# Two-stage cross-attention: two 512x512 products made from seven block products instead of eight, with mixed context sums on GpSimd and their low parts on VectorE

## What is computed

```
q = x wq^T;  k = c wk^T;  v = c wv^T
x1 = x + alpha * (softmax(q k^T / sqrt(512)) v) wo^T
g = g_w c + g_b;  phi = phi_w c + phi_b;  theta = theta_w x1 + theta_b
W = theta^T phi / 512
y = (W g^T)^T
out = bn_gamma * (w_w y + w_b - bn_mean) / sqrt(bn_var + 1e-5) + bn_beta + x1
```

## Time and profile before

| | |
|---|---|
| median of 3 runs | 388.72 us |
| profiled execution: span from first to last instruction | 386.3 us |
| outside that span, against the median | 2.4 us |
| TensorE busy | 381.0 us |
| VectorE busy | 310.8 us |
| ScalarE busy | 205.4 us |
| GpSimd busy | 3.7 us |

### The profile page before, as it was taken

How to read it: one execution, slowest core, us unless ns; L and a number is a source line. 1 busy time by engine, 2 the same in 40 slices (tenths; PEclk the granted TensorE clock), 3 DMA queues, 4 the chain that set the end, 5 groups by cost and what they waited for, 6 DMA issues and landing times.

```text
span 386.3 us, 5597 instructions
## 1 busy us (share of the span) xinstructions
PE 381.0 (99%) x1776; PEld 318.6 (82%) x1776; DVE 310.8 (80%) x595; ACT 205.4 (53%) x441; POOL 3.7 (1%) x7
## 2 busy tenths in 40 slices
PE   8999999999999999999999999999999999999995
PEld 5888878888888888888888888888888888888885
DVE  4999779987599776996689866996779875996786
ACT  3477568533664267543665257452665346552553
POOL 0001000000000000000000000000000000000000
PEclk9999999999999999999999999999999999999999
DMA  8995842486375646556383556565375564043423
GB/s 242 382 331 188 285 133 54 158 296 225 116 256 145 238 141 211 182 171 217 109 271 112 214 170 198 189 198 188 123 219 181 191 190 136 15 121 144 151 87 110
DMA packets 58059, 70.37 MB, mean 182 GB/s; under 512 B 5056, under 2 KB 47936, under 8 KB 54976
## 3 DMA queue, kind: packets, MB, share of 16 engines
q1 hardware_dynamic: 56144, 67.21, 53.2%
q10 hardware_dynamic: 1904, 3.02, 2.5%
HBM read 51.32 MB, written 18.89 MB: 182 GB/s over the span
## 4 chain that ended last, share of the span: by engine, by line
PE 97%; DMA 1%; DVE 1%; ACT 0%; issue 0%; SPq 0%
PE bank L367 23%; PE bank L368 23%; PE bank L369 23%; PE bank L421 8%; PE bank L440 7%; PE bank L407 5%; PE bank L429 4%; PE bank L462 2%; PE bank L466 1%; DMA xb<-w_k 1%; DVE xb L1143 0%; DVE xb L1138 0%; PE bank L393 0%; ACT theta_hi L621 0%; ACT t_sides L621 0%
## 5 line engine op out<-in xcount | busy, mean ns | idle before, releaser
L367 PE MATMUL bank<-ov_hi,c_sides 128*128 128x512 f32 x128 | 50.0, 391 | 0.0
L368 PE MATMUL bank<-c_sides,qk_hi 128*128 128x512 f32 x128 | 49.9, 390 | 0.0
L369 PE MATMUL bank<-c_sides,qk_lo 128*128 128x512 f32 x128 | 49.9, 390 | 0.0
L368 PE MATMUL bank<-ov_lo,c_sides 128*128 128x512 f32 x128 | 49.9, 390 | 0.0
L367 PE MATMUL bank<-c_sides,qk_hi 128*128 128x512 f32 x128 | 49.8, 389 | 0.0
L369 PE MATMUL bank<-ov_hi,c_sides 128*128 128x512 f32 x128 | 49.8, 389 | 0.0
L621 ACT ACTIVATE t_sides<-bank 128x512 fp32r<-128x512 f32 x32 | 19.0, 594 | 37.2 <-PE bank L369 37.2
L421 PE MATMUL bank<-t_sides,xT_hi 128*128 128x512 f32 x128 | 31.9, 391 | 0.0
L877 DVE TENSOR_TENSOR vo_lo<-bank,vo_hi 128x512 fp32r<-128x512 f32 x32 | 21.8, 685 | 11.8 <-ACT vo_hi L621 10.9
L621 ACT ACTIVATE probs<-bank 128x512 f32<-128x512 f32 x16 | 9.4, 585 | 37.9 <-PE bank L429 37.9
L367 PEld LDWEIGHTS bank<-ov_hi,c_sides 128*128 128x128 f32 x128 | 24.1, 188 | 5.2 <-DVE wg_sides L877 0.4
(11 more groups left out here) (148 smaller groups left out, 820.9 us busy)
## 6 DMA issues: line engine op xcount, KB each, us to landing
cT_raw<-ctx_t SPq DMA_DIRECT2D x8, 1024.0 KB, 4.8
xT_raw<-x_t SPq DMA_DIRECT2D x8, 1024.0 KB, 5.1
c_raw<-ctx_n SPq DMA_DIRECT2D x8, 1024.0 KB, 6.5
xb<-x SPq DMA_DIRECT2D x16, 512.0 KB, 4.2
out<-xb SPq DMA_DIRECT2D x14, 512.0 KB, 2.8
gram_moved<-gram_blocks SPq DMA_DIRECT2D x16, 256.0 KB, 2.3
gram_blocks<-gram_moved SPq DMA_DIRECT2D x64, 64.0 KB, 2.0
moved<-blocks SPq DMA_DIRECT2D x16, 256.0 KB, 2.3
```

Source lines behind the costliest of these rows:

```text
L367: pe.matmul(dst, ahi, bhi, start=(k == 0), stop=False)
L368: pe.matmul(dst, ahi, blo, start=False, stop=False)
L369: mm = pe.matmul(dst, alo, bhi, start=False, stop=(k == k_tiles - 1))
```

## The change

Both products are made with two-by-two blocks of 256 in seven block products, M1 to M7 (the scheme of Strassen in Winograd's form), instead of eight. The two batches of a pair stand side by side as C11, C12 (upper half of the hidden dimension, batches 0 and 1) and C21, C22 (lower half).

- qk and ov are kept as seven blocks: three pure ones and four sums, made at the start by `weight_blocks` on VectorE (seven steps for each weight) and `pure_blocks` and `sum_block` on ScalarE. The low parts of ov's sums are made on GpSimd.
- For each pair GpSimd makes four sums of context blocks, T1 = C12 - C11, N2C = T1 - C22, T3 = C22 - C12, N4C = N2C + C21 (`mixes`), in the memory of c_raw, after the context sums. ScalarE makes their high parts, VectorE their low parts (`mix_part`). Both products use them.
- Each block product is 12 matmuls of 256 columns. M1, M6, M7 and M4 accumulate in one chain bank. ScalarE copies M1 to a seed bank, to which M2 is added (`copy_chain`), and copies M5 to SBUF (`keep_join`). VectorE adds the chain to it twice: `join` writes a PSUM bank, `join_side` the side block in SBUF.
- TensorE waits for all four low parts of t before a pair. delta(0) needs three of the blocks of vo.
- x1 and vo share their memory, theta and pT too.
- load_cT waits for GpSimd's last sum, load_c for the last low part of the sums; load_c stands behind load_xT.
- At the start the high part of w_o moves from VectorE to ScalarE, and GpSimd makes the low parts of phi_w and theta_w.

The diff, cut to its core:

```diff
+FIRST_SUMS = 4
 BLOCKS = P // SQUARE
 SCALE = float(H) ** -0.5
+PRODUCTS = 7
+M1, M2, M3, M4, M5, M6, M7 = range(PRODUCTS)
+A11, A12, S4, A22, S1, N2, S3 = range(PRODUCTS)
+T1, N2C, T3, N4C = range(4)
+MIXED_SIDE = {M4: N4C, M5: T1, M6: N2C, M7: T3}
...
-        x1 = split("x1", [P, 2, KL, H])
+        x1 = vo
+        mix = split("mix", [P, 4, KS, S])
...
-        theta = split("theta", [P, 2, H])
-        qk = split("qk", [P, KH, H])
-        ov = split("ov", [P, KH, H])
+        theta = [t[:].rearrange("p b x n -> p b (x n)") for t in pT]
+        qk = split("qk", [P, PRODUCTS, KH // 2, H // 2])
+        ov = split("ov", [P, PRODUCTS, KH // 2, H // 2])
...
+        mix_raw = c_raw[:].rearrange("p b k (c s) -> p (b k) c s", c=KS)
+        sums_raw = xb[:].rearrange("p b t (c n) -> p (b t) c n", c=2)
+        side_raw = blocks[:, 1].rearrange("p j x a -> p (j x a)").rearrange("p (c n) -> p c n", c=2)
+        vo_side, tT_side = gram_raw[:, 0], probs[:, 1]
...
+        VO_CHAIN, VO_JOIN, VO_SEED = 2, 3, 6
+        TT_CHAIN, TT_JOIN, TT_SEED = 0, 1, 4
...
             load_xT(0)
+            sp.wait_ge(cT_lo, 2)
+            sp.wait_ge(mix_made, 4)
+            load_cT(1)
+            sp.wait_ge(mix_lo, 4)
             load_c(0)
...
                 if prefetch:
-                    if not first:
-                        sp.wait_ge(c_summed, four[8])
-                        load_c(p + 2)
                     sp.wait_ge(cT_lo, two[4])
-                    load_cT(p + 2)
+                    sp.wait_ge(mix_made, four[8])
+                    load_cT(ahead)
...
                     sp.wait_ge(xT_lo, two[4])
-                    load_xT(p + 2)
+                    load_xT(ahead)
+                    sp.wait_ge(mix_lo, four[8])
+                    load_c(ahead)
...
-            def t_tile(m):
-
-                product(bank[TT_BANK[m]][:].rearrange("p (b s) -> p b s", b=2), lambda k: cut(qk, every, k, tile(m)),
-                        lambda k: cut(cT, every, k),
-                        KH).then_inc(tT_done, 1)
+            def context(i, kt):
+
+                if i in MIXED_SIDE:
+                    return cut(mix, every, MIXED_SIDE[i], kt)
+                k, b = {M1: (kt, 0), M2: (2 + kt, 0), M3: (2 + kt, 1)}[i]
+                return cut(cT, every, k, b)
+
+            def half_product(dst, lhsT, rhs, opens):
+
+                for n in range(2):
+                    for kt in range(2):
+                        (ahi, alo), (bhi, blo) = lhsT(n, kt), rhs(n, kt)
+                        at = dst[:, n * S:(n + 1) * S]
+                        pe.matmul(at, ahi, bhi, start=(opens and n == 0 and kt == 0), stop=False, skip_group_check=True)
+                        pe.matmul(at, ahi, blo, start=False, stop=False, skip_group_check=True)
+                        mm = pe.matmul(at, alo, bhi, start=False, stop=(kt == 1), skip_group_check=True)
+                return mm
+
+            def t_product(i, to_bank, opens=False):
+
+                half_product(bank[to_bank], lambda n, kt: cut(qk, every, i, kt, tile(n)),
+                             lambda n, kt: context(i, kt), opens).then_inc(tT_done, 1)
+
+            def v_product(i, to_bank, opens=False):
+
+                half_product(bank[to_bank], lambda n, kt: [t[:, tile(n)] for t in context(i, kt)],
+                             lambda n, kt: cut(ov, every, i, kt), opens).then_inc(vo_done, 1)
...
-            pe.wait_ge(qk_lo, KH)
+            pe.wait_ge(qk_lo, 1)
+            pe.wait_ge(qk_summed, 4)
             pe.wait_ge(cT_lo, 2)
-            both_rows(0)
-            t_tile(0)
-            pe.wait_ge(ov_lo, 2)
-            both_rows(1)
-            pe.wait_ge(ov_lo, KH)
-            t_tile(1)
+            t_product(M1, TT_CHAIN, opens=True)
+            pe.wait_ge(qk_sum_lo, 1)
+            pe.wait_ge(mix_lo, 1)
+            t_product(M5, TT_JOIN, opens=True)
+            pe.wait_ge(tT_copied, 1)
+            pe.wait_ge(qk_sum_lo, 2)
+            pe.wait_ge(mix_lo, 2)
+            t_product(M6, TT_CHAIN)
+            pe.wait_ge(qk_lo, 3)
+            t_product(M2, FIRST_TT_SEED)
+            gram_rows(0, 0, FIRST_GRAM_BANK)
+            pe.wait_ge(tT_joined, 1)
+            pe.wait_ge(qk_sum_lo, 3)
+            pe.wait_ge(mix_lo, 3)
+            t_product(M7, TT_CHAIN)
+            pe.wait_ge(ov_lo, 3)
+            pe.wait_ge(ov_summed, 4)
+            gram_rows(0, 1, FIRST_GRAM_BANK)
+            for i in range(KS):
+                gram_rows(1, i, FIRST_GRAM_BANK)
+            pe.wait_ge(qk_sum_lo, 4)
+            t_product(M3, TT_JOIN)
+            pe.wait_ge(tT_joined, 2)
+            pe.wait_ge(mix_lo, 4)
+            t_product(M4, TT_CHAIN)
+            pe.wait_ge(wg_factor_lo, 2)
             pe.wait_ge(gram_read, 1)
-            t_tile(2)
-            pe.wait_ge(gram_read, 2)
-            t_tile(3)
-            pe.wait_ge(wg_factor_lo, 2)
-            pe.wait_ge(tT_lo, 2)
             combine_w_g()
...
-                pe.wait_ge(tT_lo, four[3])
+                two, four = counts(pe, p, 2, [1, 2, 3, 4]), counts(pe, p, 4, range(-2, 9))
+                pe.wait_ge(tT_lo, four[4])
                 pe.wait_ge(xT_lo, two[2])
-                if not first:
+                if first:
+                    pe.wait_ge(gram_read, 2)
+                else:
                     pe.wait_ge(out_made, four[-2])
-                high_scores(0, range(KH - 1))
-                pe.wait_ge(tT_lo, four[4])
-                high_scores(0, [KH - 1])
...
+                v_product(M1, VO_CHAIN, opens=True)
+                if not first:
                     pe.wait_ge(phi_turned, p + 1)
-                for st in range(KS):
-                    values(0, st)
+                v_product(M5, VO_JOIN, opens=True)
+                pe.wait_ge(vo_copied, two[1])
+                v_product(M6, VO_CHAIN)
+                v_product(M2, VO_SEED)
+                pe.wait_ge(vo_joined, two[1])
+                v_product(M7, VO_CHAIN)
...
+                pe.wait_ge(vo_joined, two[2])
+                v_product(M4, VO_CHAIN)
+                v_product(M3, VO_JOIN)
+                pe.wait_ge(vo_lo, four[3])
...
+                t_product(M1, TT_CHAIN, opens=True)
+                pe.wait_ge(mix_lo, four[5])
+                t_product(M5, TT_JOIN, opens=True)
+                pe.wait_ge(x1_made, four[4])
                 theta_rows(0, [four[1], four[2]])
-                pe.wait_ge(x1_made, four[4])
-                t_tile(1)
+                pe.wait_ge(tT_copied, two[3])
+                pe.wait_ge(mix_lo, four[6])
+                t_product(M6, TT_CHAIN)
+                t_product(M2, TT_SEED)
...
+                pe.wait_ge(tT_joined, two[3])
+                pe.wait_ge(mix_lo, four[7])
+                t_product(M7, TT_CHAIN)
...
+                pe.wait_ge(tT_joined, two[4])
+                pe.wait_ge(mix_lo, four[8])
+                t_product(M4, TT_CHAIN)
+                t_product(M3, TT_JOIN)
...
+            def copy_chain(to_bank, from_bank, done, count, copied):
+                act.wait_ge(done, count)
+                act.activation(bank[to_bank][:], bank[from_bank][:], ACT.Identity).then_inc(copied, 1)
+
+            def keep_join(side, from_bank, done, count, copied):
+                act.wait_ge(done, count)
+                act.activation(side, bank[from_bank][:].rearrange("p (n s) -> p n s", n=2), ACT.Identity).then_inc(copied, 1)
...
             act.wait_ge(ov_done, KH)
-            for m in OV_ORDER:
-                hi(ov[0][:, m, :], bank[KH + m][:], ov_hi, scale=row[:, ROW_ALPHA:ROW_ALPHA + 1])
+            mix_part(T1, 1)
+            mix_part(N2C, 2)
+            act.wait_ge(qk_summed, 4)
+            pure_blocks(ov, KH, ov_done, ov_side, ov_hi, scale=row[:, ROW_ALPHA:ROW_ALPHA + 1])
+            mix_part(T3, 3)
+            mix_part(N4C, 4)
+            copy_chain(FIRST_TT_SEED, TT_CHAIN, tT_done, 1, tT_copied)
+            keep_join(tT_side, TT_JOIN, tT_done, 2, tT_copied)
...
+                copy_chain(VO_SEED, VO_CHAIN, vo_done, seven[1], vo_copied)
                 exp(1)
-                vo_part(0, 0)
+                keep_join(vo_side, VO_JOIN, vo_done, seven[2], vo_copied)
+                if not last:
+                    c_sums(loads[32], batches=[0])
+                vo_part(0, HALF[0], VO_SEED, seven[4])
+                pT_part(0)
+                if not last:
+                    c_sums(loads[32], batches=[1])
+                vo_side_part()
+                if last:
+                    t1_part(0)
+                vo_part(0, HALF[1], VO_CHAIN, seven[6])
                 if first:
                     xT_part(0, loads[32])
-                vo_part(0, 1)
-                if first:
-                    xT_part(1, loads[32])
-                pT_part(0)
+                vo_part(1, HALF[0], VO_JOIN, seven[7])
+                pT_part(1)
...
+            def join(side, join_bank, chain_bank, done, count, kept, copied, joined):
```

(96 more changed lines are left out.)

345 lines of the change are left out of this document (175 added, 170 removed).

## The result

The changed kernel takes 445.12 us (median of 4 runs, 442.37 to 447.7) against 388.55 us before in the same batch: ratio 1.145, 95% interval 1.140 to 1.150. The direction was forecast, the size was not: 428.0 was the point and 442 the upper end of the range. The profiled execution took 442.37 us, the shortest of the four, with a span of 440.6 us, 54.3 us more than the 386.3 us before. The other three have spans of 442.8 to 444.8 us and no trace, so what they have more is not explained here.

A forecast was written before the change was run, and what follows sets the result against it. TensorE, 99% busy, was taken to bound the kernel before, VectorE and its waits after. 388.7 + 17.7 (start) + 4.6 (pair 0) + 15.1 (six steady pairs) + 1.8 (last pair) = 427.9 us; point 428, range 406 to 442.

The forecast's parts named there:

- T1 at 33.3: At the start: GpSimd's first sum follows directly behind its reduction, which ended at 31.7, and is made at 33.3 us.
- rival D: GpSimd's sums hold up VectorE's two-input SBUF steps: 0.8 to 1.6 us in 7 pairs, 2 at the start; 438 us, chance 0.17.
- the walk: Steps followed in written order; in a steady pair 40.7 us of VectorE work plus 6.0 idle give 46.7 us.
- B: Rival: waits shorter than walked, pair 45.0 us, start +11, pair 0 +3, last +1; 408 us, chance 0.18.
- C: Rival: joins hide, TensorE's floor sets the pair, 1.8 us less in 8 pairs, start +11 at most; 385.3 us, chance 0.05.
- TensorE: Both products, 84 matmuls of 256 columns each instead of 48 of 512: 1.8 us less a pair, floor 42.4 us.
- rival E: Matmuls of 256 columns cost more than 0.119 us, for example 0.14: 3.5 us a pair of TensorE; 440 us, chance 0.05.
- VectorE's amount: In a pair: eight more steps of 512 columns at 0.60 us, raising VectorE from 35.84 to 40.7 us.
- GpSimd's sum: A two-input sum of 512 columns on GpSimd: taken as 1.6 us, between 1.0 and 3.2.
- The start: Up to pair 0: GpSimd's sums behind the reduction hold ScalarE and VectorE; pair 0 starts at 59.5 instead of 41.84, +17.7 us.
- VectorE's list alone: At the start, were the GpSimd wait gone, VectorE's steps would still put pair 0 at about 53 us, +11.
- Pair 0: First pair, with t1 rows and sums in its second half: last low part of t at 50.5 against 45.9, +4.6 us.

The follow-up runs named there:

- e4: Kernel before with each tile of the two products cut from 12 matmuls of 512 columns to 21 of 256, part of the contraction left out: 380.57 us, ratio 0.980.
- e7: Kernel before with 21 matmuls of 256 columns a tile (part of the contraction left out) and eight more unused VectorE steps a pair: 396.06 us, ratio 1.018.
- e5: Changed kernel with GpSimd's pair sums cut to 2 columns and ScalarE's side block ahead of the second half of the context sums: 430.85 us, ratio 1.108.
- e2: Changed kernel with GpSimd's four sums of a pair made of 2 columns instead of 512, the rest left out: 436.27 us, ratio 1.119.
- e3: Changed kernel with ScalarE's side block moved ahead of the second half of the context sums, nothing left out: 441.91 us, ratio 1.137.
- e9: Kernel before, full-width matmuls kept, with eight more VectorE steps of 512 columns a pair whose result is unused: 398.66 us, ratio 1.026.
- e1: Changed kernel with GpSimd's reduction over partitions moved behind the sums and ov's low parts at the start, nothing left out: 433.52 us, ratio 1.119.

## Why the prediction was off

The direction was right and the sum was 17.2 us short. Three of its steps failed. The sums at the start were put right behind the reduction ("T1 at 33.3"), and it took 7.18 us more to go back to an ordinary step. GpSimd's hold-up of VectorE stood as rival D and at nothing in the sum; it costs some 4.9 us in the loop and 2.2 in pair 0. And the walk had no term for TensorE's granted clock after a long wait, which costs some 1 us at the end of the start and 1 in pair 0. Rivals B and C are out: a late pair is 47.5 us, not 45.0 or less.

**The pair, in steps.** The experiments take a late pair apart: 44.24 before; 42.68 with the narrow matmuls (e4, −1.56); 44.9 with eight steps on VectorE (e7, +2.2); 45.8 with the rest of the change, but without the hold-up and with the side block first (e5, +0.9); 46.8 with ScalarE's order as written (e2, +1.0); 47.5 with GpSimd's full sums (+0.7). The +0.9 of e5 over e7 is what is left over: the joins' waits, ScalarE's copies and the rest of the order have no experiment of their own. The steps depend on the order in which they are taken: e3 shows the side block's order worth 0.2 with the hold-up there, e5 shows it worth 1.0 without.

**TensorE** was put at −1.8 us a pair (the prediction's own 10.90 and 10.03 give 1.74); it is −1.56 where TensorE sets the time. The 0.119 us for a matmul of 256 columns held (in the steady pair after they start at 226.63, 226.75 and 226.87), so rival E is out. That the saving would be lost once VectorE is full was right, and e7 and e9 measure it: 0.8 left.

**VectorE's amount** was put at 40.7 us; the window shows 41.70. Two steps stretched from 0.69 to 1.46 and 1.49 are 1.6 us of record; e2, where they are not stretched, has 40.30 in the pair from 211.51. The step that writes PSUM, for which there had been no row, starts at 252.52 and the next at 253.12: 0.60, as taken.

**The walk through the pair** gave 6.0 us of idle time. The trace has, in the pair from 215.7, 1.92 at the scores (1.4 was walked), 0.17 for phi (1.0), 0.54 for the exponentials (0.65), 0.78 and 1.03 for the two half blocks (0.85 and 1.1), 0.32 for the product behind them (0.35), 0.35 for xT (0.65): 5.1 us. TensorE's wait before delta(0) was 1.78 (1.6), before the joined bank 0.27 (0.85). The window has 5.8 us of idle time in all (47.50 less 41.70), the small gaps included. Without the hold-up a late pair is 46.8; 46.7 was walked. That they agree so well is in part luck, since the wrong terms make up for each other: the scores cost 0.5 more, the wait for phi is there in pair 1 (1.24 us, the line below, from the same view) and has shrunk to 0.17 in the pair from 215.7.

```profile
126.72 1.14 DVE L1220 SCALAR_TENSOR_TENSOR phi_blocks<-row,c_sum,phi_blocks 128x128 f32<-128x128 f32 x4 [1.24 <-DMA phi_blocks<-phi_moved]
```

Pair 1 is 48.5 us. Over the six pairs the forecast was 2.5 us each and the measurement 3.4: 0.8 of it is the hold-up, which was in D and not in the sum.

**GpSimd's sum** was put at 1.6 us, and is 1.25 to 1.30 alone, up to 2.3 beside VectorE. The estimate of 1.1 from the Trainium skill (GPSIMD Engine Reference, Performance versus the Vector engine) was nearer to the step alone than the row of 256 columns was.

**Rival D was true** and had a chance of 0.17. I had let one row speak for GpSimd as the one that waits, since VectorE's step beside it kept its 0.69 us. The rows of before show why it did. A VectorE step with two SBUF inputs was already under way when GpSimd's began at 18.57:

```profile
18.14 0.69 DVE L877 TENSOR_TENSOR xT_lo<-c_raw,xT_hi 128x512 fp32r<-128x512 f32 x1
```

The next such step followed it without a gap and ended at 19.44. GpSimd ended at 20.17, 0.73 us later (0.74 in the changed kernel, 0.93 in e1 and e2), and 0.73 us is what a GpSimd step of 256 columns took in the changed kernel at 42.66 (that one has two inputs). So the 1.60 us read best as a wait of 0.87 and a step of 0.73; they were neither a price for GpSimd nor a sign that VectorE never waits. In the loop it is GpSimd that starts first, and then VectorE waits. The rule of the Trainium skill (SBUF — State Buffer, two separate sides), that whichever of the two starts first has the pair of ports for its whole instruction, is what the changed kernel, e1, e2 and e3 show: 1.46, 1.49 and 1.73 instead of 0.69 on VectorE, each ending 0.55 to 0.56 us after GpSimd's, and 2.3 instead of 1.3 on GpSimd. The price of 0.7 to 0.8 us in a loop pair is the low end of what D gave, that of 2.2 in pair 0 is above its high end of 1.6.

**The start** was where the forecast failed most. Its structure was right: GpSimd's sums behind the reduction, ScalarE held by T1 in front of ov's high parts (10.81 us idle), VectorE behind it. What failed is the step "The new sums stand behind it in program order: T1 at 33.3". The row of before gave a gap of 9.74 us ahead of the reduction, and I priced it as if it belonged to the first use. Nothing followed the reduction in the kernel before, so no row could show that going back costs 7.18 us again. T1 is there at 38.0, 4.7 us late, and pair 0 is 6.4 us later than walked. The other 1.7 us lie almost all at the end. VectorE has the turned sums at 61.42 where 56.4 was walked, so it has lost only another 0.3, although its steps beside GpSimd's were longer (1.13 and 1.53 us at 38.74 and 40.02 for low parts of 0.68) and although the walk's own seven steps at 0.68 from 36.2 end at 41.0 and not at 41.6. ScalarE's four issues and the w_w factor then take 2.8 us, 2.4 walked. Combining the factors takes TensorE 1.65 us, 0.7 walked: between 64.25 and 65.90 the granted clock is 0.50. That VectorE's list alone would give about 53 was tested by no run: e1 starts at 57.9, but GpSimd holds up VectorE there as well.

**Pair 0** was walked to 50.5 us and took 53.8. In it TensorE's first ten score matmuls take

```profile
65.90 4.27 PE bank L467 x10
```

in the chain, against 2.29 us before. The last window of the first table has the granted clock at 0.50, the 1.2 GHz level, after 9.5 us in which TensorE had waited for t_lo. e2 has the same program up to its pairs' sums, and its pair 0 lasts 50.7 us. From the step on u (L1220, at 91.13 and at 88.94) to the next pair's first score matmul (119.58 and 117.39) it is 28.45 us in both kernels, so all of the difference lies ahead of that step, in two places. The first is the scores. ScalarE's copy of them, in the changed kernel and then in e2:

```profile
71.25 0.60 ACT L687 ACTIVATE probs<-bank 128x512 f32<-128x512 f32 x1 [2.21 <-PE bank L475]
```

```profile
71.21 0.60 ACT L687 ACTIVATE probs<-bank 128x512 f32<-128x512 f32 x1 [0.61 <-PE bank L475]
```

Pair 0 begins 1.0 us earlier in the changed kernel, and yet the copy is no earlier: its ten score matmuls take 4.27 us against 3.29 in e2, whose first 4 us have a granted clock of 0.74. ScalarE has done with the wait for the stored sums by then (2.56 us), and it is the scores that it waits for last. So here, unlike in e1, the clock's loss is not in the shadow: it costs 1.0 us. The second place is GpSimd's sums, which in pair 0 lie beside more steps of VectorE. A sum of GpSimd and VectorE's rows, in the changed kernel and then in e2:

```profile
87.59 1.29 POOL L1417 TENSOR_TENSOR c_raw<-cT_raw 128x512 f32<-128x512 f32 x1
...
87.63 1.80 DVE L1202 TENSOR_TENSOR pT_lo<-probs,pT_hi 128x512 fp32r<-128x512 f32 x1
89.36 1.85 DVE L1159 TENSOR_TENSOR row<-row,phi_rows 128x256 f32<-128x256 f32 x2
```

```profile
87.67 0.68 DVE L1202 TENSOR_TENSOR pT_lo<-probs,pT_hi 128x512 fp32r<-128x512 f32 x1
88.27 0.75 DVE L1159 TENSOR_TENSOR row<-row,phi_rows 128x256 f32<-128x256 f32 x2
```

With the side block's low part (1.38 against 0.71 us) they put the step on u 2.2 us later. The two places make up the 3.2 us between the kernels, and e2's 50.7 is what was walked. The walk's 50.5 had neither.

**The range** ended at 442, which was D's 438 and little more. The changed kernel has D's hold-up (6 x 0.8 = 4.9 us), a start 6.4 us and a pair 0 3.3 us beyond their points: 14.6 us on 427.9 gives 442.5, the profiled execution's 442.37 (the loop has another 0.6, and the time outside the span is 0.6 less). The other three executions took 444.55 to 447.7. I had bounded the start by GpSimd's price alone and had pair 0 as a point, and had let no two of them go wrong together.

## What to carry to other kernels

An idea that saves work on the full engine by giving work to the next fullest is priced by the sum of both lists, not by the slack between their busy times: here 8.4 us of slack a pair did not hide eight steps of 0.6 us, which cost 1.5 us with nothing else changed. A gap that waits for nothing, next to an unusual operation on an engine, should be priced twice, once into it and once back, before anything is queued behind it. And before elementwise work goes to GpSimd, look at which VectorE steps with two SBUF inputs it will stand beside, and which of the two will start first: a row in which the one did not wait says nothing of the other order.

## What the runs showed of the hardware

- GpSimd's reduction over partitions has a gap ahead of it (9.74 us before, 7.58 after, 5.85 in e1; 5.75 to 10.46 over all kernels) and the next ordinary step another of 7.18 us (6.66 to 7.18). The profile has no releaser for them but "issue"; what the engine does in them no run shows.
- A GpSimd sum of 512 columns with two SBUF inputs takes 1.25 to 1.30 us when it does not meet a VectorE step with two SBUF inputs that is already under way, and 1.6 to 2.3 us when it does. A VectorE step of 0.69 us that starts during such a sum became 1.38 to 1.80, and in five rows (two in the pair from 215.7, two in pair 0, one in e3) it ended 0.55 to 0.56 us after the sum.
- Sums of 2 columns on GpSimd, four of them one behind another, took 0.65 us together in e5 and in pair 0 of e2, some 0.16 us each. In the loop pairs of e2 they took 1.13; a two-input step of VectorE (227.32, 0.69) lies beside them there.
- A matmul of 256 columns costs 0.119 us against 0.227 for 512, where the granted clock is 1.00: halving the columns saves 48%, not 50%. At a granted clock of 0.50 (64.62 to 65.48 in the changed kernel) those of 256 start about 0.21 us apart.
